# Block moves split evenly between two DMA queues: those that read partitions 64 to 127 issued by ScalarE behind its exponentials

## What is computed

```python
q = (M @ Wq.T).reshape(e, h, dh).transpose(1, 0, 2)
kv = x @ Wkv.T + bkv
k, v = jnp.split(kv, 2, axis=-1)
...
sim = jnp.einsum('hid,hjd->hij', q, k) * dh ** (-0.5)
sim = jnp.where(mask, sim, -1000000000.0)
attn = jax.nn.softmax(sim, axis=-1)
out = jnp.einsum('hij,hjd->hid', attn, v)
out = out.transpose(1, 0, 2).reshape(e, h * dh)
out = out @ Wo.T + bo
m = layer_norm(out + M)
ffn = jax.nn.relu(m @ W1.T + b1) @ W2.T + b2
z = layer_norm(ffn + m)
```

## Time and profile before

| | us |
|---|---|
| median of 3 runs | 763.78 (762.9 to 764.46) |
| the profiled execution | 757.08 |
| its span, first to last instruction | 754.7 |
| DVE busy in the span | 552.9 |
| PE busy | 648.0 |
| ACT busy (issuing DMAs not counted) | 366.1 |

### The profile page before, as it was taken

How to read it: one execution, slowest core, us unless ns; L and a number is a source line. 1 busy time by engine, 2 the same in 40 slices (tenths; PEclk the granted TensorE clock), 3 DMA queues, 4 the chain that set the end, 5 groups by cost and what they waited for, 6 DMA issues and landing times.

```text
span 754.7 us, 11237 instructions
## 1 busy us (share of the span) xinstructions
PE 648.0 (86%) x3382; PEld 401.9 (53%) x3382; DVE 552.9 (73%) x688; ACT 366.1 (49%) x658; POOL 243.4 (32%) x293
## 2 busy tenths in 40 slices
PE   4867989898898989898989989898989659799995
PEld 3654545554455555455555445554545315578884
DVE  4496799778986898779987899689977732534333
ACT  4454555546555555455564555555554411333332
POOL 2221542227320532245222632054222430522223
PEclk9978999999999999999999999999999869799998
DMA  7066599857896689849986799668874981022221
GB/s 289 1 174 144 126 222 246 221 138 178 216 263 145 148 214 256 187 106 222 249 225 146 172 219 263 144 150 206 211 171 122 301 217 45 28 92 103 83 83 56
DMA packets 52504, 127.96 MB, mean 170 GB/s; under 512 B 15744, under 2 KB 16256, under 8 KB 52224
## 3 DMA queue, kind: packets, MB, share of 16 engines
q1 hardware_dynamic: 41728, 101.97, 52.6%
q10 hardware_dynamic: 10752, 25.70, 13.5%
HBM read 23.80 MB, written 1.05 MB: 33 GB/s over the span
## 4 chain that ended last, share of the span: by engine, by line
PE 49%; SPq 17%; DVE 13%; issue 8%; DMA 8%; ACT 3%; POOL 0%; DVEq 0%; ACTq 0%; POOLq 0%
SPq L335 16%; PE tail L831 12%; PE slot L804 10%; PE tail L729 9%; DVE st L658 7%; DMA pt<-st 7%; PE slot L882 6%; PE slot L890 6%; PE slot L729 5%; DVE prob L648 3%; ACT val L519 1%; DMA wq_raw<-in_wq 1%; PE slot L763 1%; PE tail L838 1%; DVE stats L682 1%
## 5 line engine op out<-in xcount | busy, mean ns | idle before, releaser
L513 ACT ACTIVATE prob<-prob,negmax 128x896 f32<-128x896 f32 x224 | 233.7, 1043 | 239.5 <-DVE negmax L648 236.4
L648 DVE CUSTOM_DVE_ANT_0 prob<-slot,lower,negmax_old 128x896 f32<-128x896 f32 x224 | 249.0, 1149 | 77.8 <-PE slot L804 68.7
L658 DVE STREAM_TRANSPOSE st<-prob 128x1792 f32<-128x1792 f32 x112 | 228.5, 2041 | 22.1 <-DMA pt<-st 20.4
L831 PE MATMUL tail<-pt,val 128*64 128x512 f32 x784 | 191.0, 622 | 20.5 <-DMA pt<-st 10.3
L804 PE MATMUL slot<-k_hi,q_hi 64*128 64x448 f32 x448 | 98.0, 429 | 34.8 <-DVE negmax L648 34.8
L831 PEld LDWEIGHTS tail<-pt,val 128*64 128x64 f32 x784 | 52.2, 142 | 125.3 <-issue 105.7
L804 PEld LDWEIGHTS slot<-k_hi,q_hi 64*128 64x128 f32 x448 | 44.6, 190 | 101.9 <-issue 93.8
L804 PE MATMUL slot<-k_hi,q_lo 64*128 64x448 f32 x448 | 87.4, 379 | 0.0
L804 PE MATMUL slot<-k_lo,q_hi 64*128 64x448 f32 x448 | 86.8, 377 | 0.0
L413 POOL TENSOR_TENSOR total<-total,alpha 128x8 f32<-128x8 f32 x28 | 5.7, 205 | 225.3 <-ACT alpha L550 225.3
L426 POOL TENSOR_TENSOR k_lo<-k_raw,k_hi 128x896 fp32r<-128x896 f32 x27 | 57.0, 2110 | 3.9 <-POOL k_hi L423 0.2
(11 more groups left out here) (110 smaller groups left out, 832.1 us busy)
## 6 DMA issues: line engine op xcount, KB each, us to landing
pt<-st SPq DMA_DIRECT2D x672, 112.0 KB, 3.0
pt<-st ACTq DMA_DIRECT2D x224, 112.0 KB, 3.4
w_raw<-in_w SPq DMA_DIRECT2D x32, 256.0 KB, 2.8
x_raw<-in_x SPq DMA_DIRECT2D x6, 896.0 KB, 5.8
mask_raw<-in_mask SPq DMA_DIRECT2D x7, 448.0 KB, 5.3
mt_raw<-in_mt SPq DMA_DIRECT2D x2, 512.0 KB, 7.8
wq_raw<-in_wq SPq DMA_DIRECT2D x2, 512.0 KB, 8.5
wo_raw<-in_wo SPq DMA_DIRECT2D x1, 1024.0 KB, 5.5
```

The source lines that it names most:

```text
L513: nc.scalar.activation(unit, unit, ACT.Exp, bias=negmax[:, p, u:u + 1], scale=-1.0, accum_out=psumrow[:, p, u:u + 1]).then_inc(exp_done, 1)
L648: nc.vector.tensor_tensor_reduce(out=prob[:, i % 2, h].rearrange("p (b n) -> p b n", b=2), in0=slot[:, j, :, :HALF], in1=lower[:, i].rearr ...
L658: nc.vector.transpose(st[:, g].rearrange("p b k (t i) -> p k b t i", t=2)[:, :, :, t2], prob[:, i % 2].rearrange("p h (k b i) -> p (h k) b ...
L831: last = nc.tensor.matmul(outT[DH * h:DH * h + DH], val[:, i, head(p, h)], moving, start=(i == 0), stop=(i == KT - 1))
```

## The change

Each side now issues 8 of the 16 moves of a g. SyncE has those that read partitions 0 to 63 (`SP_MOVES`), ScalarE those that read 64 to 127 (`ACT_MOVES`). ScalarE's 8 are cut in four parts of two. In the list of steps, `B000` is part 0 of g = 0, `B010` part 1, `B020` part 2 and `B031` part 3 of g = 0 for the pair before; `B101` to `B131` are the same for g = 1. Part 0 stands right behind E0, parts 1 and 2 behind E1 of the same round, part 3 behind E0 of the next round. Only part 0 waits on semaphores. In round 3 of pair 2, where W6 and C stand late, parts 0 to 2 come together at the end.

```diff
+SP_MOVES = ((0, 0), (1, 2), (0, 1), (1, 3), (0, 2), (1, 0), (0, 3), (1, 1))
+ACT_MOVES = ((2, 2), (3, 0), (2, 3), (3, 1), (2, 0), (3, 2), (2, 1), (3, 3))
...
-    ('S E0 E1 W0 W1 W2 W3 X M1',
-     'S E0 V0 E1 Z K H L X B1',
-     'S E0 E1 F W4 W5 W6 C A X M0',
-     'S E0 V1 E1 V2 V3 X B0'),
-    ('S E0 V4 E1 W0 W1 W2 X M1',
-     'S E0 E1 Z F K H L A X B1',
-     'S E0 V5 E1 W3 W4 W5 X M0',
-     'S E0 V6 E1 W6 C X B0 J I'),
...
+    ('S E0 B031 E1 W0 W1 W2 W3 X M1',
+     'S E0 B101 V0 E1 B111 B121 Z K H L X',
+     'S E0 B131 E1 F W4 W5 W6 C A X M0',
+     'S E0 B000 V1 E1 B010 B020 V2 V3 X'),
+    ('S E0 B031 V4 E1 W0 W1 W2 X M1',
+     'S E0 B101 E1 B111 B121 Z F K H L A X',
+     'S E0 B131 V5 E1 W3 W4 W5 X M0',
+     'S E0 V6 E1 W6 C X J I B000 B010 B020'),
...
-        out.extend([("X", b, 3), ("M", b, 1), ("B", b, 1), ("Z", b, 0)])
+        out.extend([("X", b, 3), ("M", b, 1), ("B", b, (0, 3)), *(("B", b, (1, k)) for k in range(4)), ("Z", b, 0)])
...
-                        for turn in (0, 1, 2):
-                            for a in (0, 2, 1, 3):
-                                b = (a + turn) % QUAD
-                                sp.dma_start(pt[LANES * b:LANES * b + LANES, buf, a],
-                                             st[LANES * a:LANES * a + LANES, i, b]).then_inc(landed[buf], 16)
+                        for a, b in SP_MOVES:
+                            sp.dma_start(pt[LANES * b:LANES * b + LANES, buf, a],
+                                         st[LANES * a:LANES * a + LANES, i, b]).then_inc(landed[buf], 16)
...
+                        g, part = i
+                        buf = move_buf(p, g)
+                        if part == 0:
+                            read = in_register(act, KT * (n - 1)) if is_past(n, 2) else None
+                            written = in_register(act, QT * n + 2 * g + 2)
+                            act.wait_ge(zeroed, 2)
+                            if read is not None:
+                                act.wait_ge(pv_done, read)
+                            act.wait_ge(xposed, written)
+                        for a, b in ACT_MOVES[2 * part:2 * part + 2]:
+                            act.dma_start(pt[LANES * b:LANES * b + LANES, buf, a],
+                                          st[LANES * a:LANES * a + LANES, g, b]).then_inc(landed[buf], 16)
```

More of the change, by code:

```diff
@@ L92, in chunk_schedule @@
                     step = (kind, p + 1, i)
-                elif kind in "MB":
+                elif kind == "M":
                     step = (kind, p - i, i)
+                elif kind == "B":
+                    step = (kind, p - i % 10, (i // 100, i // 10 % 10))
                 elif kind == "Z":
@@ L535, in body @@
                     if kind == "B":
-                        buf = move_buf(p, i)
-                        read = in_register(act, KT * (n - 1)) if is_past(n, 2) else None
-                        written = in_register(act, QT * n + 2 * i + 2)
-                        act.wait_ge(zeroed, 2)
-                        if read is not None:
-                            act.wait_ge(pv_done, read)
-                        act.wait_ge(xposed, written)
-                        for turn in (3,):
-                            for a in (0, 2, 1, 3):
-                                b = (a + turn) % QUAD
-                                act.dma_start(pt[LANES * b:LANES * b + LANES, buf, a],
-                                              st[LANES * a:LANES * a + LANES, i, b]).then_inc(landed[buf], 16)
+                        g, part = i
[10 more added lines that the diff above has]
+                                          st[LANES * a:LANES * a + LANES, g, b]).then_inc(landed[buf], 16)
                     if kind == "Z":
```

## The result

| | before | after |
|---|---|---|
| median of 4 runs, us | 763.34 (762.62 to 764.46) | 788.25 (784.58 to 794.0) |
| the profiled execution, us | 757.08 | 789.34 |
| its span, us | 754.7 | 787.6 |

The ratio is 1.034 (95% interval 1.028 to 1.039): 3.4% slower. That is outside my range of 757 to 771, and on the side to which I gave 0.30. Each kernel ran beside the one of before, whose median went from 762.0 to 765.0 us, so runs are best compared by their ratios.

A forecast was written before the change was run, and what follows sets the result against it. VectorE was taken as the bound from pair 3 to the end of pair 1, TensorE from there through pair 2. Terms -8.0 + 4.3 + 2.0 - 1.0 + 2.6 = -0.1 us gave 763.7 us, range 757 to 771.

The forecast's parts named there:

- Nothing else moves the sum: All remaining steps, including SyncE's loads I, R (x) and Q coming earlier into free buffers, were put at 0 us.
- First loss, V2: Round 3 of pair 1: moves ahead of V2's copy make V3 0.6 us later in each of 7 chunks, 4.3 us.
- Second loss, V5: Round 2 of pair 2: two moves ahead of V5's copy start W5 0.3 us late in each chunk, 2.0 us.
- First gain, pair 3: First transpose of pair 3: sooner issue was to remove waits for moves, 4.1 of 5.5 us counted.
- Second gain, pair 1: First transpose of pair 1: sooner issue was to remove waits for moves, 3.9 of 5.15 us counted.
- The last chunk: Long wait for SyncE's moves 1.0 us shorter; four more ScalarE moves ahead of `ao_hi` delay the output projection 2.6 us.
- slower, by full DMA engines: Waits at first transposes of pairs 1 and 3 stay, losses stand alone: 772.7 us, 768 if half stay; chance 0.30.
- Its sign: Slower rival's turning point: it decides the sign once less than 6 of the 10.7 us of waits go.

The follow-up runs named there:

- E0: Not a run: the step in ScalarE's list that is the first exponential of a round; it has no measured time or ratio as a kernel.
- run 5: Changed kernel, with SyncE's load of the next chunk's x moved from round 0 of pair 0 to round 2 of pair 1; 782.04 us, ratio 1.027.
- run 14: Changed kernel, but in pair 0 ScalarE's last two moves of the second buffer are issued by SyncE ahead of the load of x; 786.41 us, ratio 1.030.
- run 6: Kernel before the change, with the load of x moved from round 0 of pair 0 to round 2 of pair 1; 757.75 us, ratio 0.994.
- run 7: As run 6, and in the last chunk SyncE issues its moves of pair 2 ahead of the late weights; 759.89 us, ratio 0.997.
- run 8: Changed kernel with value copies ahead of the moves, x loaded later and the late weights loaded later; 760.23 us, ratio 0.996.
- run 11: Changed kernel with value copies ahead of moves, x loaded later, and four of ScalarE's last eight moves put behind the copy of outT_sb; 760.15 us, ratio 0.995.
- run 10: Kernel before the change, its 12 to 4 split kept, ScalarE's four moves in round 3 of pair 1 put among the value copies; 772.86 us, ratio 1.014.
- run 13: Kernel before the change, with the last two of ScalarE's four moves in pair 0, round 1 put behind round 2's first exponential; 767.62 us, ratio 1.008.
- run 9: Changed kernel, with four of ScalarE's eight last moves in the last chunk put behind the copy of outT_sb; 785.2 us, ratio 1.020.
- run 2: Changed kernel, with ScalarE's last two moves of pair 0's second buffer pulled from round 2 into round 1; 798.24 us, ratio 1.048.
- run 3: Changed kernel, with each queue's eight moves alternating between partitions 0 to 63 and 64 to 127; 811.53 us, ratio 1.048.
- run 1: Changed kernel, with all value copies put ahead of the moves, so none stands between an exponential and a value copy; 769.55 us, ratio 1.010.
- run 4: Changed kernel, with ScalarE's eight moves issued in one go at the ends of rounds 3 and 1, behind the value copies; 811.16 us, ratio 1.066.
- run 12: As run 11, but each queue takes its moves from both halves of the partitions in turn; 765.06 us, ratio 0.999.

## Why the prediction was wrong

The forecast was 763.7, the result 788.25 us, 24.6 apart. In the profiled execution the sum was off by 33.0 us, and that splits so.

*"Nothing else moves the sum ... the SyncE loads I, R and Q come earlier into buffers that are free."* This step failed worst: 11.3 us with what follows. I asked whether x's buffer was free and not which moves its 896 KB share the DMA engines with. The profile before had a hint: the waits of pair 1 lay behind the load of x, and I read them as a matter of issue order. Runs 5 and 14 show the cause: the two last moves issued behind the load. With the load elsewhere (run 5) or these two ahead of it (run 14) the wait in round 3 of pair 0 is gone. "What follows" is TensorE: it waits for the same moves and runs at the lower clock behind the three large ones, so that VectorE then waits 0.3 to 1.5 us for scores in round 0 of pair 1.

*First loss, V2: 0.6 us a chunk, 4.3 us.* The mechanism was right, the term mis-sized. V2's copy starts 331.09 - 326.73 = 4.36 us after its E0 in chunk 3 (4.1 forecast, 3.4 before), and the round grows by 0.9 us, 6.4 in seven. The other 5.2 us are what the three chunks with a low clock lose on top, 4.6 of them in chunks 1 and 6; chunk 0 had the low clock before as well. I never asked what TensorE's longer gap does to its clock, although has the clock as a column.

*Second loss, V5: 2.0 us.* Measured 2.5.

*First gain, pair 3: 4.1 of 5.5 us.* It did not come; that round lost 2.6 us, 2.2 of them in the first two chunks. The windows of the changed kernel ahead of the wait at 282.60 show why:

```profile
275.00:278.00 3.00, 3.00 (x20) 1.29 (x18) 3.00 (x5) 0.73 (x1) 2.37 (x2) 1.00 1.04 268
278.00:281.00 3.00, 3.00 (x20) 2.56 (x19) 2.87 (x4) 2.39 (x5) 0.00 (x0) 1.00 1.08 259
```

The DMA engines are at a share of 1.04 to 1.08 and 259 to 268 GB/s, much as they were with twelve and four moves. The issue did get shorter, and the landing did not move. In chunk 2 the sixteen are issued from 273.12 on, the last at 277.31 + 0.54 = 277.85, that is 4.7 us after the first, where it was 6.9:

```profile
273.12 6.30 SPq L338 DMA_DIRECT2D pt<-st  x9
273.24 3.89 ACTq L549 DMA_DIRECT2D pt<-st  x6
277.31 1.16 ACTq L549 DMA_DIRECT2D pt<-st  x2
```

(Eight of the nine are M0's.) The transpose that waits for the last starts 282.60 - 273.12 = 9.48 us after the first issue. Before it was 264.78 - 255.30 = 9.48 us, the same. I had given the last move a median landing of 3.4 us; it took 4.6. My own numbers said as much: 7.3 us of data against 6.9 us of issue, and I still called the issue the slower of the two. That is the mechanism of my slower rival: sixteen moves take their time whoever issues them. The rule of the Trainium skill that I had weighed ("DMA: Bandwidth & Descriptors", "Issuing engines are not separate DMA queues": a second issuer saves only issue time) described this place better than my sum; I had taken three quarters of the gain against it.

*Second gain, pair 1: 3.9 of 5.15 us.* The waits for moves went in all chunks, but only 1.2 us came. In chunks 3 and 5, which had no large wait in pair 0, the moves land 1.3 to 1.8 us sooner and the round is 1.5 and 1.4 us shorter, as forecast. In chunks 1, 2 and 4, behind the new waits, VectorE waits 1.2 to 1.3 us for scores instead. Run 6 gets 3.0 us there in chunks 1 to 5 by moving x alone: the wait was the load's.

*The last chunk: -1.0 and +2.6 us.* The landing did not come sooner but 12.74 - 11.38 = 1.4 us later, although SyncE issued its last move earlier. The 2.6 us are as forecast. The 1.7 us of clock behind them were missing.

Of the rivals, "slower, by full DMA engines" had the waits of pair 3 right. Its price, 772.7 at most, was too low by what it did not have: x beside the moves, and the clock. (Its sign, by my own terms, turns when less than 7.9 of the 10.7 us go, 4.3 + 2.0 + 2.6 - 1.0, not less than 6.) For the range I had varied the prices of steps that I saw, and left no room for a step that I had put at nothing.

## What to carry to other kernels

Before a transfer's issue moves by two microseconds, list what else is in flight at its new time, above all one large load on the other queue, and who needs the small ones that travel beside it. When issues go onto a compute engine, keep them behind every copy that TensorE waits for: here each cost the next instruction 0.65 us, and a round that was due to lose 0.9 us lost up to 3.3, through TensorE's clock. A cost put at zero belongs into the range with its worst case, and an experiment that moves a transfer needs a look at the issue times before its result is read. The fastest version here is the kernel before with the load of x moved (run 6, 757.75 us, 0.994); runs 7, 8 and 11, at 0.995 to 0.997, can't be told from it.

## What the runs showed of the hardware

TensorE's clock fell to 0.50 behind gaps ahead of V2 of 1.9 to 3.8 us (the changed kernel, runs 10, 11, 13 and 14) and stayed at 1.00 behind others of up to 3.24 us (run 10, chunk 3). In none of the profiled executions did it fall there behind one of 1.83 us or less. Length alone does not decide, and the same program differs from chunk to chunk and from one execution to the next: up to its last burst run 9 is the changed kernel, and it had the low clock behind V2 in five of chunks 1 to 6 where that one had it in two. A fall costs 2.2 to 2.7 us where V3 runs at the lower clock too (the changed kernel, runs 10, 11 and 13), and 1.0 us where the clock is back at 1.00 by V3 (runs 2 and 9).

Chance alone does not explain it. In chunks 1 to 6 of the kernels that have moves among the copies of V1 and V2 (the changed one, runs 2, 3, 5, 9, 10 and 14) the clock was low behind V2 in 22 of 42 chunks; in the others (the kernel before, runs 1, 4, 6, 7, 8, 11, 12 and 13) in 4 of 54. Three of these four are in run 13, where only moves of another round were shifted; what set them off is not settled.

In chunks 1, 2 and 4 of the changed kernel the load of 896 KB took 7.2 to 8.9 us, where it had taken 5.4 to 6.4 in the kernel before, and the two moves issued 0.8 to 1.5 us behind it landed in 5.2 to 8.2 us, where a move takes 3.5. In chunks 3 and 5, with the same order of issue, the load took 5.5 and 5.6 us and these moves 5.0 to 5.3.
